# Layer 0's expert products from fp32 to three fp32r terms, with the weights split in place, in a four-stage expert kernel

## The reference, cut to what matters

```
x = x + 0.5 * ffn0(layernorm(x))     # 8 experts, top 2, width 176, and a shared MLP of width 352
x = x + mix0(layernorm(x))           # time mixing and channel mixing of layer 0
x = x + 0.5 * ffn0(layernorm(x))
x = x + 0.5 * ffn1(layernorm(x))     # 32 experts, top 6, width 96, and a shared MLP of width 192
x = x + attn1(layernorm(x))
x = x + 0.5 * ffn1(layernorm(x))

# ffn of one row: sum over its chosen experts e of weight[e] * (silu(x @ w_gate[e]) * (x @ w_up[e])) @ w_down[e], plus the shared MLP
```

## Time and profile before

| | us |
|---|---|
| median of 3 runs | 1366.76 |
| lowest and highest | 1365.97, 1370.21 |
| profiled execution, its time | 1363.16 |
| span from first to last instruction | 1361.3 |
| TensorE busy / GpSimd busy / VectorE busy | 1136.8 / 583.4 / 753.1 |
| mean granted TensorE clock | 0.914 |

### The profile page before, as it was taken

One profiled execution on the slowest core, in us unless ns is written; L12 is line 12 of the kernel. 1 busy time (PEld: TensorE's weight loads), 2 busy tenths in 40 slices (PEclk: granted clock), 3 DMA queues, 4 the chain that ended last, 5 costly groups with the idle time before them and its releaser, 6 DMA issues.

```text
span 1361.3 us, 19456 instructions
## 1 busy us (share of the span) xinstructions
PE 1136.8 (84%) x5926; PEld 924.3 (68%) x5926; DVE 753.1 (55%) x2317; ACT 487.6 (36%) x936; POOL 583.4 (43%) x571
## 2 busy tenths in 40 slices
PE   4999996688898998997465599999988584999993
PEld 3776774456677886775353499998564563999993
DVE  5763365636455653366524184767777542656665
ACT  3422343374454422343231144444242311444441
POOL 3670243221112221227777302667507776006675
PEclk9899998898898999998577799999998687999997
DMA  9622435910000047743322567887302223568986
GB/s 326 262 71 84 142 104 189 334 37 1 0 1 32 32 179 270 256 136 126 126 100 94 192 187 218 276 265 236 106 1 93 98 97 115 161 191 272 283 278 203
DMA packets 125154, 210.03 MB, mean 154 GB/s; under 512 B 15280, under 2 KB 104752, under 8 KB 123184
## 3 DMA queue, kind: packets, MB, share of 16 engines
q1 hardware_dynamic: 100480, 141.64, 31.2%
q0 software_dynamic: 24576, 67.14, 15.6%
HBM read 129.56 MB, written 101.19 MB: 170 GB/s over the span
## 4 chain that ended last, share of the span: by engine, by line
PE 56%; POOL 12%; DVE 12%; issue 10%; ACT 5%; DMA 4%; SPq 0%; ACTq 0%; POOLq 0%; DVEq 0%
PE ps L828 16%; PE ps L838 11%; POOL xd L588 10%; PE ps L746 5%; PE ps L799 5%; PE ps L758 4%; PE ps L1105 3%; PE ps L809 3%; PE ps L971 2%; POOL G L602 2%; PE ps L978 2%; ACT xnt L1213 2%; DMA G<-yd,slot_of 1%; PE ps L887 1%; DMA yd<-yo 1%
## 5 line engine op out<-in xcount | busy, mean ns | idle before, releaser
L602 POOL DMA_INDIRECT G<-yd,slot_of x256 | 249.6, 975 | 356.4 <-DMA yd<-yo 255.4
L588 POOL DMA_INDIRECT xd<-xnt,slot_of x256 | 254.7, 995 | 185.9 <-DVE slot_of L1754 102.0
L828 PE MATMUL ps<-WE,xT 128*128 x1016 | 190.3, 331 | 0.3
L1348 ACT ACTIVATE xT<-ps 128x512 f32<-128x512 f32 (+1 forms) x168 | 99.3, 591 | 213.8 <-PE ps L799 213.6
L1864 DVE TENSOR_TENSOR hid<-hid,ps 128x192 f32<-128x192 f32 (+2 forms) x168 | 65.4, 389 | 183.9 <-ACT hid L1367 183.2
L828 PEld LDWEIGHTS ps<-WE,xT 128*128 128x128 f32 x1016 | 165.7, 194 | 1.1 <-issue 0.9
L1843 DVE SCALAR_TENSOR_TENSOR XT<-G,wt,XT 128x256 f32<-128x256 f32 x256 | 124.7, 488 | 45.0 <-DMA G<-yd,slot_of 32.8
L1871 DVE COPY yo<-ps 128x512 f32<-128x512 f32 (+1 forms) x168 | 114.8, 684 | 61.3 <-PE ps L838 61.3
L799 PE MATMUL ps<-ident,xd_in 128*128 128x128 f32 x664 | 103.4, 278 | 37.4 <-DMA xd_in<-xd 31.3
L838 PE MATMUL ps<-WE,hT 96*128 x508 | 130.8, 380 | 0.0
L1232 ACT ACTIVATE S<-ps 128x512 f32<-128x512 f32 (+1 forms) x72 | 42.8, 595 | 242.0 <-PE ps L746 237.4
(11 more groups left out here) (225 smaller groups left out, 1886.8 us busy)
## 6 DMA issues: line engine op xcount, KB each, us to landing
xd_in<-xd SPq DMA_DIRECT2D x164, 256.0 KB, 3.9
yd<-yo SPq DMA_DIRECT2D x164, 256.0 KB, 3.0
WE<-w SPq DMA_DIRECT2D x8, 1280.0 KB, 6.8
W0E<-w0e SPq DMA_DIRECT2D x2, 4864.0 KB, 24.1
xd<-xnt,slot_of POOLq DMA_INDIRECT x256, 2.4
G<-yd,slot_of POOLq DMA_INDIRECT x256, 3.9
XT<-x_in SPq DMA_DIRECT2D x4, 512.0 KB, 5.8
out<-XT SPq DMA_DIRECT2D x16, 128.0 KB, 3.4
```

The costliest lines, as they stand in the source:

```text
L588: nc.gpsimd.indirect_dma_start(xd[f // 2][:, :], bass.IndirectOffsetOnAxis(ap=slot_of[:, t, k:k + 1], axis=0), xnt[:, t, :], None).then_in ...
L602: nc.gpsimd.indirect_dma_start(G[:, n % G_RING, :], None, yd[f // 2][0:min(ly.early[t] * 2, ly.TILES) * P, :], bass.IndirectOffsetOnAxis(a ...
L828: last = mm(dst, xT[:, q % 2, a, k, :], flat[:, bass.ds(expert[2 * q + a] + k * 2 * ly.H, 2 * ly.H)], start=(k == 0), stop=(k == KD - 1))
L1348: fn(xT[:, q % 2, 0:m].rearrange("p a k t -> p (a k t)"), ps[:, TX, 0:m * D], ACT.Copy).then_inc(TL.xT, 1)
```

## The change

It concerns layer 0's two tile stages, f = 0 and 1 (`HALVED`).

- Each fp32 product in `up` and `down_rows` becomes three fp32r products: high rows times high weights, high rows times low weights, low rows times high weights. That is 12 matmuls in `up` of a full pair (352 columns) and 12 in `down_rows` (256 columns) in place of 4 and 4 in fp32.
- The weight table is split twice, ahead of f = 0 and of f = 1. ScalarE copies an expert's 1216 columns to the high table W0H (`expert_high`, 8 times), GpSimd subtracts it from W0E in place into W0L (`expert_low`, 8 times). `up` of the first pair waits for all eight. Ahead of f = 1 GpSimd does its eight between scatter(1, 2) and scatter(1, 3), and ScalarE its eight after chunks 3 to 6 of DRAIN.
- ScalarE's copies of the transposes give the high parts; VectorE makes the low parts (`x_low`, `h_low`) from the PSUM bank less the high part, and each bank is free only then. The copy to `yo` moves from VectorE to ScalarE (`finished`).
- `down_rows` runs two pairs behind, over PSUM banks 7 and 6. TensorE's order is: transpose q+1, hooks `ahead`, `up(q)`, hidden transpose q-1, `down_rows(q-2)`, hooks `between`. On ScalarE and VectorE all hooks come after the pair's own steps.
- The splits of the eight WH pieces move from before f = 0 to the beginning of the mixing: three after the last gather of f = 0, two after the difference of block 1, three after block 0's residual sum.
- The second load of W0E starts earlier, as its place is free earlier. Five of the eight loads of layer 1's expert weights move behind f = 1. Buffers and the banks of f = 2's early routing move; the tile stages f = 2 and 3 keep their work.

```diff
@@ SyncE
-            for i in range(SPLIT0, SPLIT1):
-                sp.dma_start(raw_wa[i - SPLIT0][:, :], pieces[i][0]).then_inc(wa_in, 16)
...
             tiles(0)
+            sp.wait_ge(TL.down, PAIR0[1])
+            for i in range(SPLIT0, SPLIT1):
+                sp.dma_start(raw_wa[i - SPLIT0][:, :], pieces[i][0]).then_inc(wa_in, 16)
...
             sp.wait_ge(CK.gu, RUN["c", 3][0][-1].i + 1)
-            sp.wait_ge(CK.gu, RUN["s", 1, 1][0][-1].i + 1)
-            sp.wait_ge(F_NORM[1].lo, 2)
-            sp.wait_ge(RT.logits, 4 + 2)
             sp.wait_ge(A0.crm, NB)
             sp.dma_start(W0E[:], w0e).then_inc(w0e_in, 16)
@@ GpSimd
+            def expert_low(l, e):
+                pool.wait_ge(ew_hi, LY[0].E * l + e + 1)
+                nc.gpsimd.tensor_tensor(W0L[:, e, :], W0E[:, e, :], W0H[:, e, :].bitcast(F32), ALU.subtract).then_inc(ew_lo, 1)
+
+            for e in range(LY[0].E):
+                expert_low(0, e)
...
+            for h in range(3):
+                channel_weights(h)
             for s in range(1, STAGES):
...
                     difference(b1, 0, A0.dl1)
+                if s == 1:
+                    channel_weights(3)
+                    channel_weights(4)
...
-            for b in range(STAGES - 4, NB):
-                scatter(1, b)
+            scatter(1, NB - 2)
+            for e in range(LY[0].E):
+                expert_low(1, e)
+            scatter(1, NB - 1)
@@ TensorE, up (down_rows likewise, with hTh, hTl and 256 columns)
+                    if f in HALVED:
+                        pe.wait_ge(TL.xlo, q + 1)
+                        for a in range(ly.tiles_in(i)):
+                            for k in range(KD):
+                                at = bass.ds(expert[2 * q + a] + k * 2 * ly.H, 2 * ly.H)
+                                dst = ps[:, bank + a, 0:2 * ly.H]
+                                mm(dst, xTh[:, q % 2, a, k, :], flat_hi[:, at], start=(k == 0), stop=False)
+                                mm(dst, xTh[:, q % 2, a, k, :], flat_lo[:, at], start=False, stop=False)
+                                last = mm(dst, xTl[f][:, q % 2, a, k, :], flat_hi[:, at], start=False, stop=(k == KD - 1))
@@ ScalarE, tiles
+                    gate(q)
+                    if q > q0:
+                        hturned(q - 1)
+                    if between:
+                        between(q - q0)
+                    if f in HALVED and q > q0 + 1:
+                        finished(q - 2)
                     if beside:
                         beside(q - q0)
@@ ScalarE, ahead of f = 0 in chunk k, ahead of f = 1 in DRAIN
+                    if 3 <= k < 3 + LY[0].E:
+                        expert_high(0, k - 3)
...
+                    if 3 <= d < 3 + LY[0].E // 2:
+                        expert_high(1, 2 * (d - 3))
+                        expert_high(1, 2 * (d - 3) + 1)
@@ VectorE, tiles
+                if f in HALVED:
+                    x_low(q0)
                 for q in range(q0, q1):
+                    if f in HALVED:
+                        if q + 1 < q1:
+                            x_low(q + 1)
+                    gated(q)
+                    if f in HALVED and q > q0:
+                        h_low(q - 1)
                     if ahead:
                         ahead(q - q0)
-                    gated(q)
```

More of the change, by code:

```diff
@@ L179, in program @@
         XT = sb("XT", [P, TT, D], F32)
+        xnt_at = place[0]
         xnt = sb("xnt", [P, TT, D], F32)
@@ L202, in program @@
         xt_at = tb_at + 4 * X_RING * 2 * D
[L203 to L208, removed]
+        hi_end = wh_at + 4 * LY[0].E * LY[0].EW
+        W0H = sb("W0H", [P, LY[0].E, LY[0].EW], F32R, wh_at)
+        W0L = sb("W0L", [P, LY[0].E, LY[0].EW], F32R, r1_at)
         inside, upto = area(s_at)
@@ L536, in _ @@
                 sp.dma_start(stage1[:, c, :], wsh1[c]).then_inc(sh1_in, 16)
+            for g in range(2, 7):
+                expert_group(g)
             def attention_weights(i):
@@ L582, in scatter_tile @@
                 if t == 0 and f % 2 == 0:
-                    pool.wait_ge(filled[f // 2], 16 * (-(-ly.ROWS // NTOK)))
+                    pool.wait_ge(filled, 16 * sum(-(-LY[l].ROWS // NTOK) for l in range(f // 2 + 1)))
                 if t % NT == 0:
@@ L614, in _, with channel_weights @@
                 scatter(0, b)
-            pool.wait_ge(wa_in, 16 * HID)
-            for i in range(SPLIT0, SPLIT1):
-                _, dst, start, n = pieces[i]
-                split(i, raw_wa[i - SPLIT0][:, :], dst, start, n)
-            pool.wait_ge(w_ready, SPLIT1)
+            def expert_low(l, e):
[3 more added lines that the diff above has]
+                expert_low(0, e)
+            def channel_weights(h):
+                pool.wait_ge(wa_in, 16 * HID)
+                _, dst, start, n = pieces[SPLIT0 + h]
+                split(SPLIT0 + h, raw_wa[h][:, :], dst, start, n)
             def difference(b, which, done):
@@ L652, in _ @@
                     nc.gpsimd.tensor_tensor(XT[:, tiles_of(b2), :], XT[:, tiles_of(b2), :], XA[:, b2 % 2], ALU.add).then_inc(A0.xx, 1)
+                if s == 1:
+                    for h in range(5, HID):
+                        channel_weights(h)
                 if b1 + 1 < NB:
@@ L833, in down_rows @@
                     pe.wait_ge(TL.hT, q + 1)
-                    pe.wait_ge(TL.y, freed(f, q))
+                    pe.wait_ge(TL.y, max(q - 1, q0))
                     ty = down_bank(f, q)
+                    if f in HALVED:
+                        pe.wait_ge(TL.hlo, q + 1)
+                        for a in range(ly.tiles_in(q - q0)):
+                            for c in range(ly.parts):
+                                at = bass.ds(expert[2 * q + a] + ly.down_at + c * D, D)
+                                dst, n = ps[:, ty, a * D:(a + 1) * D], a * ly.parts + c
+                                mm(dst, hTh[0:ly.part, q % 2, n, :], flat_hi[0:ly.part, at], start=(c == 0), stop=False)
+                                mm(dst, hTh[0:ly.part, q % 2, n, :], flat_lo[0:ly.part, at], start=False, stop=False)
+                                last = mm(dst, hTl[f][q % 2][0:ly.part, n, :], flat_hi[0:ly.part, at], start=False, stop=(c == ly.parts - 1))
+                        last.then_inc(TL.down, 1)
+                        return
                     for a in range(ly.tiles_in(q - q0)):
@@ L1249, in shared, with expert_high @@
                 hidden(chunks[-1])
+            def expert_high(l, e):
+                if e == 0:
+                    act.wait_ge(w0e_in, 16 * (l + 1))
+                    if l == 1:
+                        act.wait_ge(CK.down, RUN["c", NB - 1][0][-1].i + 1)
+                if l == 0 and e == 6:
+                    act.wait_ge(CK.gu, RUN["s", 0, 0][0][-1].i + 1)
+                fn(W0H[:, e, :], W0E[:, e, :], ACT.Copy).then_inc(ew_hi, 1)
             def first_prepare():
@@ L1893, in tiles @@
                         beside(q - q0)
-                for q in range(q1 - lag, q1):
-                    rows(q)
+                if f in HALVED:
+                    h_low(q1 - 1)
+                else:
+                    for q in range(q1 - lag, q1):
+                        rows(q)
                 return done[0]
```

195 lines of the change are left out of this document (121 added, 74 removed).

## The result

The changed kernel takes 1396.03 us (median of 4 runs, 1392.93 to 1399.73), the kernel before beside it 1367.39 (1365.97 to 1370.21): ratio 1.0212, interval 1.0186 to 1.0237. It is 2.1% slower; 1368 (1355 to 1381) was forecast. The spans differ by 1393.7 - 1361.3 = 32.4 us.

What follows compares the result with a forecast made beforehand. TensorE's own work bounds f = 0 and early f = 1, GpSimd's list the part behind. Terms -5.8 + 2.5 + 2.7 + 7.5 - 6.0 = +0.9 on the median 1366.8 gave 1368 us, range 1355 to 1381.

Steps and rivals of the forecast that it cites:

- The matmuls: Tile steps of f = 0 and 1: 0.65 us saved a step, 4.32 for 4.97, bounds 0.75 and 0.
- Addressed products can't follow: Rival, tile steps: 24 register-addressed products a step miss 119 ns; at 200 ns +45, about 1412; chance 0.08.
- the price of the exclusion: Preparations and mixing: a VectorE operation with two SBUF inputs loses up to one GpSimd instruction, 2.75 us for a new subtraction.
- The two preparations: Weight-table splits: ahead of f = 0 +2.5 us (+1 to +5), in DRAIN +7.5 (+3 to +12).
- one group can get in between two of them: DRAIN: chosen(1, 3)'s four groups each pass between two GpSimd subtractions, +10.7 us; two groups per gap, +4.6.
- Both are covered, with about 1 us to spare for a VectorE hook: Steps of f = 0: ScalarE some 2.3 and VectorE some 3.1 of 4.3 us, so TensorE still sets the pace.
- The loads come some 8 us ahead of the need: Mixing: loads for the split WH pieces come after the last down, some 8 us before they are needed.
- The mixing +2.7: Moved split pairs: first three cost 0, next two +1.2, last three +1.5 us; bounds +0.5 and +5.
- f = 1 -6: Second tile stage: block 1's route_stats come about 6.5 us earlier, GpSimd's list unchanged; -6 us, bounds -8 and -2.
- the list of 149 us behind it: Behind f = 1: GpSimd's gathers and scatters, from last norm to f = 2, stay at 149 us.
- all good ends: Sum of the favourable bounds of all terms, put at -14 us; all bad ones +26.
- Full exclusion: Rival: each group of chosen waits a whole 2.75 us, TensorE returns at lower clock; +8, 1375 to 1377; chance 0.21.

Runs made afterwards that it cites:

- e1: Changed kernel with GpSimd waiting for its own result after each expert_low subtraction; 1610.8 us, ratio 1.0104 to the kernel before.
- e2: Changed kernel with each expert_low subtraction cut into two of 608 columns, no wait between them; 1615.3 us, ratio 1.0116 to the kernel before.
- e4: Changed kernel with the loads of WH's pieces and WSQ held back until f = 0's last gather is summed; 1613.6 us, ratio 1.0146 to the kernel before.
- e12: e9 with DRAIN's eight VectorE subtractions placed ahead of scatter(1, 3); 1359.6 us against 1367.3 for the kernel before, ratio 0.9934.
- e11: Kernel before the change with one edit, weighed(0) ahead of the gather sums left after f = 0; 1580.9 us, ratio 1.0061.
- e3: Changed kernel with the sixteen expert_low subtractions on VectorE instead of GpSimd; 1594.4 us, ratio 1.0103 to the kernel before.
- e9: Changed kernel: subtractions on VectorE, DRAIN's spread over chunks; hooks earlier; weighed(0) ahead of gather sums; gates made in pair 19; 1555.2 us, ratio 0.9911.
- e6: Changed kernel with ScalarE's hooks ahead of finished(q - 2) and three VectorE hooks ahead of the gather sums; 1594.4 us, ratio 1.0079 to the kernel before.

## Why the prediction was wrong

- **The matmuls: right.** 160 and 120 ns, also with 24 addresses in a step. The step is 4.23 us, for 4.32 predicted, at the bound of 0.75. "Addressed products can't follow" is out.
- **The step that failed: the price of the exclusion, "up to one GpSimd instruction for each such VectorE instruction".** The two preparations were put at +2.5 and +7.5, and measured +11.5 and +17.0. One `HL` ahead of f = 0 took 12.09 us beside a run of four subtractions, and one in DRAIN 13.84 beside six. The row behind the price was `HL` at 1.45: there, among splits of two alternating kinds (the second waits for the first), it got in at the next boundary. In `expert_low`, eight equal instructions in a row, it did not; e1 shows that a wait behind each lets it in, e2 that shorter pieces don't. DRAIN's own picture for `chosen`, "one group can get in between two of them", came out in e1 and e2. What it put at nothing, and without a reason, was the `HL` ahead of `chosen`: 13.2 of the 17.0 us. The Trainium skill ("SBUF — State Buffer", § Who interferes with whom) says that the two engines exclude each other for the whole instruction. I took it as one instruction per wait, and the runs show several.
- **With one instruction per wait DRAIN was short too.** Only the four groups of `chosen(1, 3)` were counted, 10.7 us at most. In e1 the two `HL` ahead of them (2.67 and 3.20 us) wait as well, and DRAIN costs 15.3 us.
- **f = 0: a second step that failed, "Both are covered, with about 1 us to spare for a VectorE hook".** -5.8 was predicted up to `weighed(0)`, +6.0 measured (-0.9 and +6.9). The terms that were named came out; the losses that were not named turned the sum. Predicted and found: 0.7 for `x_low(0)`, 2.4 ahead of `up(15)` (2.3), 2.1 ahead of `up(19)` (1.8), 13.3 for 11.7 from the steps. Missed: the wait for `xTl` (3.9). The prediction added up VectorE's time per step (3.1 of 4.3 us), but a queue in order also waits, and `x_low` stands in that queue now. Missed too: the lower clock behind that wait (3.8) and, at the end, two more gathers (2.5) and the loads beside them (3.1 by e4). "The loads come some 8 us ahead of the need" looked only at who needs them, not at what they run beside.
- **The mixing +2.7, f = 1 -6, the list of 149 us behind it: right** (+2.9, -5.1, 149.1). GpSimd's list did pass on f = 1's gain whole. One sum on record is off: all good ends together give -12, not -14.
- **Rivals.** "Full exclusion" came nearest, with the right side and the lower clock behind the wait, but it was priced at 1375 to 1377 with one instruction for each wait and no `HL` in DRAIN. The loss outgrew it.

Sum as measured: +11.5 - 0.9 + 6.9 + 2.9 - 0.2 + 17.0 - 5.1 = +32.1, against +0.9 on record. That the matmuls' gain is real is shown by the step itself. It reaches the whole in e12, 0.7% faster than the kernel before with the same products: most of its gain is in the stretch up to `up(19)` (-10.3) and f = 1 (-4.9), and the one edit of e12 that was tried on the kernel before, `weighed(0)` (e11), brought nothing there.

## What to carry over

Before work is put on an idle GpSimd, look at whether its instructions will be ready back to back, and at every VectorE operation with two inputs in SBUF in that time: a wide one can wait out the whole run, and TensorE with it, while small ones waited for one instruction at a time. What decides between the two is open. If VectorE has the room, it does the work itself in half the time. And when a queue gets an operation that TensorE waits for, look at what stands in front of it and for what that waits (gather sums, hooks), not at the queue's busy time.

## What the hardware showed

- One VectorE subtraction of 512 columns took 12.09, 13.84 and 14.25 us beside runs of 4, 6 and 12 GpSimd instructions, 0.68 alone. In the same traces operations of 8 to 32 columns got in between two instructions of a run (1.81 us in the changed kernel; 0.49, 1.40, 1.33 and 1.32 in e2). With a wait of GpSimd behind each instruction (e1) `HL` took 2.67 and 3.20 us.
- It goes the other way too: an indirect DMA's issue on GpSimd took 1.81 to 2.83 us beside VectorE subtractions with both inputs in SBUF (e3, e9), 0.96 otherwise; with one subtraction left beside them (e12) one issue of eight was long.
- fp32r matmuls with a register's address: 160 ns at 352 columns, 120 at 256, three in a row on the same PSUM region without a gap.
- After 3.9 us of idle TensorE the next 8 matmuls of a projection took 5.73 us for 3.6, with a granted clock of 0.62 from 205 to 211 us; with a wait of 0.72 us (e6) 3.60.
